# Softmax probabilities divided by their row sums on VectorE before they are turned, in a fused attention and mixture-of-experts layer

## The reference

```python
x = x + attn(layernorm(x))       # 16 heads, latent rank 64, rotary part 64
x = x + ffn(layernorm(x))        # 8 experts, 2 per token, and a shared one

# attn, per sequence b and head h
scores  = einsum('bthd,bshd->btsh', q, k) * SCALE
weights = softmax(scores, axis=2)            # over s
attn    = einsum('btsh,bshd->bthd', weights, v)
out     = attn.reshape(b, s, NH * DV) @ Wout
```

## Time and profile before

| | us |
|---|---|
| median of 3 runs (632.36 to 633.71) | 633.29 |
| the profiled execution's own time | 640.3 |
| its span (first to last instruction) | 638.6 |
| PE busy in the span | 611.4 (96%) |
| DVE busy | 469.9 (74%) |
| ACT busy | 474.8 (74%) |
| POOL busy | 410.1 (64%) |
| mean granted TensorE clock | 0.974 |

### The profile page before, as it was taken

The page is one execution under the profiler, slowest core; times in us unless marked ns, Lnnn a source line. Parts: engine busy times, 40 slices in busy tenths (PEclk is TensorE's granted clock), DMA queues, the critical chain, the costliest instruction groups (busy, mean ns, idle before and its releaser), DMA issues. The chain is left out here.

```text
span 638.6 us, 15728 instructions
## 1 busy us (share of the span) xinstructions
PE 611.4 (96%) x4916; PEld 596.4 (93%) x4916; DVE 469.9 (74%) x1406; ACT 474.8 (74%) x1331; POOL 410.1 (64%) x455
## 2 busy tenths in 40 slices
PE   9988999999999999999999999999988889999995
PEld 8878999999999999899999999999978879999994
DVE  6666787877886888778688788778755666666486
ACT  4669899898998989779898898979854335565531
POOL 1466797786897889679789988978603204444500
PEclk9997999999999999999999999999989689999997
DMA  9891000000001001000100100011403055444292
GB/s 254 254 332 29 2 1 3 2 2 34 10 10 42 10 18 44 8 16 5 43 18 10 43 9 19 34 53 43 149 1 133 33 152 166 131 119 133 77 316 87
DMA packets 34024, 45.41 MB, mean 71 GB/s; under 512 B 4056, under 2 KB 29112, under 8 KB 33944
## 3 DMA queue, kind: packets, MB, share of 16 engines
q1 hardware_dynamic: 29160, 34.56, 17.2%
q0 software_dynamic: 3408, 9.34, 4.5%
q10 hardware_dynamic: 1376, 0.50, 0.3%
HBM read 27.57 MB, written 16.82 MB: 70 GB/s over the span
## 5 line engine op out<-in xcount | busy, mean ns | idle before, releaser
L1244 ACT ACTIVATE probs<-ps_s,nmax 128x256 f32<-128x256 f32 x256 | 118.9, 475 | 14.4 <-DVE nmax L1434 14.3
L1779 POOL TENSOR_TENSOR qswap<-qswap,qsin 128x512 f32<-128x512 f32 x64 | 83.2, 1300 | 45.6 <-ACT qswap L1221 45.6
L226 PE MATMUL ps_q<-xa,wq_hi 128*128 128x256 f32 x512 | 101.0, 295 | 4.3 <-DVE qf L1429 4.3
L1434 DVE TENSOR_REDUCE nmax<-ps_s 128x2 f32<-128x512 f32 x128 | 86.9, 679 | 11.1 <-PE ps_s L226 10.6
L1221 ACT ACTIVATE pT_hi<-ps_t 128x512 fp32r<-128x512 f32 x128 | 76.6, 598 | 19.6 <-PE ps_t L978 18.2
L1782 POOL TENSOR_TENSOR qf<-qf,qswap 128x512 f32<-128x512 f32 x64 | 82.7, 1293 | 12.9 <-DVE qf L1429 8.9
L1786 POOL TENSOR_TENSOR q_lo<-qf,q_hi 128x512 fp32r<-128x512 f32 x64 | 83.0, 1297 | 6.7 <-ACT q_hi L1221 6.6
L226 PEld LDWEIGHTS ps_q<-xa,wq_hi 128*128 128x128 f32 x512 | 79.9, 192 | 6.0 <-DVE qf L1429 4.0
L299 DVE TENSOR_TENSOR pT_lo<-ps_t,pT_hi 128x512 fp32r<-128x512 f32 x128 | 81.9, 681 | 0.0
L226 PE MATMUL ps_s<-kT_hi,q_hi 128*128 128x256 f32 x256 | 78.3, 306 | 2.1 <-ACT probs L1244 2.1
L978 PE MATMUL ps_t<-ident,probs 128*128 128x128 f32 x512 | 78.0, 275 | 1.3 <-DVE pT_lo L299 1.2
(11 more groups left out here) (337 smaller groups left out, 1924.1 us busy)
## 6 DMA issues: line engine op xcount, KB each, us to landing
xg<-routed_in SPq DMA_DIRECT2D x39, 129.0 KB
normal_turned<-xf SPq DMA_DIRECT2D x8, 512.0 KB, 2.8
wq_raw<-Wq_dram SPq DMA_DIRECT2D x16, 192.0 KB, 4.6
x<-x_dram SPq DMA_DIRECT2D x8, 256.0 KB, 4.9
xa<-normal_turned SPq DMA_DIRECT2D x4, 512.0 KB, 4.8
mgu_hi<-routed_out SPq DMA_DIRECT2D x4, 512.0 KB, 5.2
mgu_lo<-routed_out SPq DMA_DIRECT2D x4, 512.0 KB, 8.0
out_dram<-x SPq DMA_DIRECT2D x8, 256.0 KB, 2.9
```

The source lines that it names most:

```text
L226: last = nc.tensor.matmul(out, stat, mov, start=start and n == 0, stop=stop and n == len(terms) - 1, skip_group_check=skip)
L1244: last = nc.scalar.activation(probs[h % 3][:, j, :], L.ps_s[h % 2][:, j, :], ACT.Exp, bias=nmax[:, h % NH, j:j + 1], accum_out=rsum[:, h % ...
L1434: vec.tensor_reduce(nmax[:, h % NH, :], L.ps_s[h % 2][:, :, :], AX.X, ALU.max, negate=True).then_inc(ev.max_done, 1)
L1779: gp.tensor_tensor(qs, qs, L.qsin[:, :].unsqueeze(1).to_broadcast([P, 2, S]), ALU.mult).then_inc(ev.qrot_part, 1)
```

## The change

`spread`, `norms` and `norm_out` fall away, and with them the tiles rinv and norm. A new function `scale(h)` on DVE multiplies the probabilities of a head in place, before PE turns them, by the reciprocal of each row's sum, which now is one number per partition. `scale` is two TENSOR_SCALAR operations of 128 x 256 in SBUF (one per tile of tokens), so four per pair. `turn(h)` waits for `scaled` in place of `exp_done`. `attended` is now a plain copy of ps_o to on, made by ACT; its place on ACT is behind `exps(2g+1)`. The first `attend` of a pair waits for `on_done` of the pair before.

```diff
             def turn(h):
-                pe.wait_ge(ev.exp_done, h + 1)
+                pe.wait_ge(ev.scaled, h + 1)
                 if h >= 2:
                     pe.wait_ge(ev.plo_done, h - 1)
...
                 pe.wait_ge(ev.plo_done, h + 1)
-                if n == 0:
-                    pe.wait_ge(ev.norm_done, g + 1)
+                if h == 0:
+                    pe.wait_ge(F.wlo_done, NH)
+                if n == 0 and g >= 1:
+                    pe.wait_ge(ev.on_done, g)
...
-            def norms(g):
-
-                if g == 0:
-                    pe.wait_ge(F.wlo_done, NH)
-                pe.wait_ge(ev.rinv_done, g + 1)
-                if g >= 1:
-                    pe.wait_ge(ev.on_done, g)
-                for j in range(NT):
-                    last = nc.tensor.transpose(L.ps_o[:, 1, tile(j)], rinv[g % 2][:, j, :, :].rearrange("p n c -> p (n c)"), L.ident[:, :])
-                last.then_inc(ev.norm_full, 1)
...
-            def norm_out(g):
-                act.wait_ge(ev.norm_full, g + 1)
-                if g >= 1:
-                    act.wait_ge(ev.on_done, g)
-                copy(norm[:, :], L.ps_o[:, 1, :]).then_inc(ev.norm_done, 1)
+            def attended(g):
+                act.wait_ge(ev.pv_done, 2 * g + 2)
+                if g >= 2:
+                    act.wait_ge(ev.olo_done, g - 1)
+                copy(on[g % 2][:, :], L.ps_o[:, 0, :]).then_inc(ev.on_done, 1)
...
-            def spread(g):
-
+            def scale(h):
+
+                g, n = divmod(h, 2)
                 dve.wait_ge(ev.small_inv, g + 1)
-                if g >= 2:
-                    dve.wait_ge(ev.norm_full, g - 1)
-                vec.tensor_reduce(rinv[g % 2][:, :, :, :].rearrange("p j n c -> p (j n) c"),
-                                  rinv_1[g % 2][:, :, :].rearrange("p j n -> p (j n)").unsqueeze(2).unsqueeze(3).to_broadcast([P, 2 * NT, RANK, 1]),
-                                  AX.X, ALU.max).then_inc(ev.rinv_done, 1)
+                for j in range(NT):
+                    last = vec.tensor_scalar(probs[h % 3][:, j, :], probs[h % 3][:, j, :], rinv_1[g % 2][:, j, n:n + 1], None, ALU.mult)
+                last.then_inc(ev.scaled, 1)
...
-            def attended(g):
-                dve.wait_ge(ev.pv_done, 2 * g + 2)
-                dve.wait_ge(ev.norm_done, g + 1)
-                if g >= 2:
-                    dve.wait_ge(ev.olo_done, g - 1)
-                vec.tensor_tensor(on[g % 2][:, :], L.ps_o[:, 0, :], norm[:, :], ALU.mult).then_inc(ev.on_done, 1)
...
                 if pair(g + 3):
                     query_cos(g + 3)
-                if pair(g - 2):
-                    attended(g - 2)
                 inverse(g)
                 if pair(g + 1):
                     maxima(2 * (g + 1))
-                spread(g)
+                scale(2 * g)
+                scale(2 * g + 1)
                 if pair(g - 1):
                     probs_lo(2 * (g - 1))
                     probs_lo(2 * (g - 1) + 1)
```

More of the change, by code:

```diff
@@ L75, in __init__ @@
             sem, ("q_full", "qraw_done", "qcos_done", "qrot_part", "qrot_done", "qhi_done", "qlo_done"))
-        self.small_inv, self.rinv_done, self.norm_full, self.norm_done, self.on_done, self.ohi_done, self.olo_done, self.out_done = map(
-            sem, ("small_inv", "rinv_done", "norm_full", "norm_done", "on_done", "ohi_done", "olo_done", "out_done"))
+        self.small_inv, self.scaled, self.on_done, self.ohi_done, self.olo_done, self.out_done = map(
+            sem, ("small_inv", "scaled", "on_done", "ohi_done", "olo_done", "out_done"))
         self.s_full, self.max_done, self.exp_done = map(sem, ("s_full", "max_done", "exp_done"))
@@ L797, in loop @@
             rinv_1 = [at(f"rinv_1{n}", [P, NT, 2]) for n in range(2)]
-            rinv = [at(f"rinv{n}", [P, NT, 2, RANK]) for n in range(2)]
-            norm = at("norm", [P, S])
             on = [at(f"on{n}", [P, S]) for n in range(2)]
@@ L1149, in _ @@
                     query(g + 4)
-                if pair(g - 1):
-                    norms(g - 1)
                 if pair(g + 1):
@@ L1162, in _ @@
             project(PAIRS - 3)
-            norms(PAIRS - 1)
             attend(HEADS - 2)
@@ L1350, in _ @@
                 exps(2 * g + 1)
+                if pair(g - 2):
+                    attended(g - 2)
                 if pair(g + 2):
@@ L1358, in _ @@
                     exps(2 * (g + 1))
-                if pair(g - 1):
-                    norm_out(g - 1)
                 if r == 4 and batch(i - 1):
@@ L1377, in _ @@
                 probs_hi(2 * g)
+            attended(PAIRS - 2)
             probs_hi(HEADS - 1)
             attended_hi(PAIRS - 2)
-            norm_out(PAIRS - 1)
+            attended(PAIRS - 1)
             silu(0, 0)
@@ L1439, in inverse @@
                 if g >= 2:
-                    dve.wait_ge(ev.rinv_done, g - 1)
+                    dve.wait_ge(ev.scaled, 2 * g - 2)
                 vec.reciprocal(rinv_1[g % 2][:, :, :], rsum[:, 2 * p:2 * p + 2, :].rearrange("p n j -> p j n")).then_inc(ev.small_inv, 1)
-            def spread(g):
+            def scale(h):
+                g, n = divmod(h, 2)
                 dve.wait_ge(ev.small_inv, g + 1)
-                if g >= 2:
-                    dve.wait_ge(ev.norm_full, g - 1)
-                vec.tensor_reduce(rinv[g % 2][:, :, :, :].rearrange("p j n c -> p (j n) c"),
-                                  rinv_1[g % 2][:, :, :].rearrange("p j n -> p (j n)").unsqueeze(2).unsqueeze(3).to_broadcast([P, 2 * NT, RANK, 1]),
-                                  AX.X, ALU.max).then_inc(ev.rinv_done, 1)
+                for j in range(NT):
+                    last = vec.tensor_scalar(probs[h % 3][:, j, :], probs[h % 3][:, j, :], rinv_1[g % 2][:, j, n:n + 1], None, ALU.mult)
+                last.then_inc(ev.scaled, 1)
             def probs_lo(h):
@@ L1696, in _ @@
                     maxima(2 * (g + 1) + 1)
-            attended(PAIRS - 2)
             probs_lo(HEADS - 2)
@@ L1701, in _ @@
             masks(B - 2)
-            attended(PAIRS - 1)
             unit_lo(0, 0)
```

## The result

The changed kernel takes 726.44 us (median of 4 runs, 725.83 to 728.19), beside 633.50 for the kernel before in the same session: a ratio of 1.144 [1.1395, 1.1485]. It is slower by 93 us; 714 was predicted, in a range from 622 to 745.

The account below looks back on a forecast made before the run. PE was taken to bound the loop before, DVE after: 3.63 own round + 1.08 scales + 1.73 waits = 6.44 us, 63 times, plus 91.8 = 497.5, 81 above 416.5; 640.3 + 81 = 721, less 7.0 gives 714 us, range 622 to 745.

Parts of the forecast that it names:

- A scale of 0.27 us from start to start: On DVE: 0.21 for a CAST-like operation plus 0.06 for the per-partition factor, 1.08 us a round.
- Waits of 1.73 us a round: DVE's scales wait for POOL's rotate 0.21, query_lo 1.25, attended_lo 0.70, less 0.43 of issue; chance 0.65.
- the upper bound: Scales' waits on DVE: 3.0 us a round, if one more POOL operation of 1.3 us gets in.
- The term for `attended_lo`, 0.70: On DVE: the third scale of a round waits 0.70 us for POOL's attended_lo, which follows query_lo at once.
- the lower end of 0.95 us a round: Scales' waits for POOL without the third, giving 665 us, the low end of the turn-taking case's own range.
- DVE's loop of 497.5 us: Attention loop on DVE: 63 rounds of 6.44 us plus 91.8 of other sequences' pieces, 81 above 416.5.
- PE waits at `turn`, 1 to 2 us a round: Expected sign in the profile after: PE waits for DVE before turn, one to two us a round.
- The mean of a scale, about 0.75 us: Expected sign on DVE: 256 TENSOR_SCALAR averaging about 0.75 us, some of 1.3 to 1.5 ending with a POOL operation.
- The final step, 721 less 7 us: Whole kernel: profiled execution 640.3 + 81 = 721, taken as 7.0 above the median, so 714 us.
- The rival "out of the fast mode": On DVE: the per-partition factor prevents the fast mode, no meeting with POOL, 1.56 us a round; 630 us, chance 0.15.
- the room of 1.52 us: On DVE: scales may take 1.52 us a round, waits included, before the loop exceeds the earlier 416.5 us.
- The gain as built, 13.3 us: PE saves 0.21 us a round from norms, 13.3 us in all, with the rest hidden; 620 us.

Follow-up runs that it names:

- no division: The changed kernel without scale, turn waiting for small_inv and the probabilities left undivided; 616.02 us, ratio 0.9699.
- POOL short: The changed kernel with POOL's rotate and query_lo operations cut to 8 columns a head, the rest left out; 625.11 us, ratio 0.984.
- sums written: The changed kernel with each scale also writing its row sum into a tile nobody reads; 661.37 us, ratio 1.0425.
- sums written, ahead of query_cos: The changed kernel with row-sum-writing scales of heads 2g-1 and 2g first in DVE's round, a reciprocal per head; 659.51 us, ratio 1.0397.
- plain, ahead of query_cos: The changed kernel with its scales, for heads 2g-1 and 2g, moved ahead of query_cos, a reciprocal per head; 672.34 us, ratio 1.056.
- sums written, in the gap: The 661.37 us kernel with scale(2g-1) behind query_cos, scale(2g) behind maxima(2g+2), a reciprocal per head; 667.16 us, ratio 1.0495.
- sums written, split: The 661.37 us kernel with scale(2g) ahead of maxima(2g+2) and scale(2g+1) behind it; 672.26 us, ratio 1.0586.
- plain, at the round's end: The changed kernel with its scales, for heads 2g+1 and 2g+2, moved to the end of DVE's round ahead of maxima(2g+3); 691.39 us, ratio 1.088.
- query_lo short: The changed kernel with only POOL's query_lo cut to 8 columns a head, the rest left out; 668.11 us, ratio 1.0528.
- attended_lo short: The changed kernel with only POOL's attended_lo cut to 8 columns, the rest left out; 705.08 us, ratio 1.1108.
- one TENSOR_TENSOR a head: The changed kernel with one 128 x 512 TENSOR_TENSOR per head, factors read with step 0, replacing two TENSOR_SCALAR; 721.01 us, ratio 1.1351.
- plain, in the gap: The changed kernel's scales without sums, scale(2g-1) behind query_cos, scale(2g) behind maxima(2g+2), a reciprocal per head; 732.90 us, ratio 1.1533.

## Why the prediction was right, step by step

The forecast was slower, and the mechanism that it named is the one that the runs show; the size of the sum came out right in part by errors that cancelled. The kernels can be laid side by side by the scales' busy time a round (times as measured; the kernel before took 633.5 to 636.6 us beside them):

| kernel | scales, us a round | us |
|---|---|---|
| no division | 0 | 616.0 |
| POOL short | 1.18 | 625.1 |
| sums written | 1.67 | 661.4 |
| sums written, ahead of query_cos | 1.68 | 659.5 |
| plain, ahead of query_cos | 1.71 | 672.3 |
| sums written, in the gap | 1.74 | 667.2 |
| sums written, split | 1.75 | 672.3 |
| plain, at the round's end | 1.78 | 691.4 |
| query_lo short | 1.80 | 668.1 |
| attended_lo short | 2.47 | 705.1 |
| one TENSOR_TENSOR a head | 2.60 | 721.0 |
| the change | 2.79 | 726.4 |
| plain, in the gap | 3.13 | 732.9 |

- **A scale of 0.27 us from start to start.** Right: four free ones take 1.14 us, three pitches of 0.27 and a last record of 0.34.
- **Waits of 1.73 us a round.** Measured 1.65. The mechanism is shown by the three kernels that take it away (another form, POOL short, `query_lo` short), and in the round above it stands as it was drawn: the rest of the rotate, `query_lo`, `attended_lo`, one free. But the composition was not that in every round. In the timelines `query_lo` begins inside 53 of the 64 trains of four (58 with those that it precedes by less than 0.2 us, which is how the expectation of the `query_lo` run counts) and `attended_lo` inside only 29, while 16 trains hold one more half of a rotate, which I had only in the upper bound. The term for `attended_lo`, 0.70, came to 0.32; that the extra rotates about made up for it was not tried, but in any case this sum was partly luck. Two of its figures were also off in the working: half of 0.27 three times is 0.41, not 0.43, and the lower end of 0.95 us a round is not "without the third wait", which by the same sum leaves 1.2.
- **DVE's loop of 497.5 us.** Measured 503.2, but made up otherwise. The sum held 461.6 us of work and one gap a round, before `inverse`, of 1.77 - 1.20 = 0.57 us, or 35.9 in all. The gap is there, 35.0 us before the RECIPROCAL, but DVE is busy for only 446.0: from start to start the scales hold 169.4 us where the sum had 177.0, and all else 276.6 where it had 284.6. Against these 16 us less stand 22 us of idle time that the sum put at nothing, before `query_cos` and `maxima` above all. So the 5.7 us between 497.5 and 503.2 are the rest of two larger errors.
- **PE waits at `turn`, 1 to 2 us a round.** 72.6 / 63 = 1.15. ACT's and POOL's shares fell, as foreseen. PE's granted clock fell from 0.99 to 0.97 in the loop, and with it PE's busy time rose from the 406.9 of the form without waits (clock 1.00) to 419.3. PE has idle time to cover it, so I put nothing on it.
- **The mean of a scale, about 0.75 us.** 0.757, with some at 1.3 to 1.46.
- **The final step, 721 less 7 us.** This one failed. The profiled execution of the kernel before lay 7.0 above its median; that of the kernel after is 726.82, level with its median of 726.44. The offset belonged to that one execution and should not have been carried over. Outside the loop the two executions take the same (640.3 - 416.5 = 223.8 and 726.8 - 503.2 = 223.6 us), so it probably lay in the loop of before, which the sum had replaced. Of the 12 us missed, 7 are here and 6 in the loop, less 1 of rounding.
- **The rival "out of the fast mode".** Its mechanism didn't occur, but the form that writes sums is as good as that case: no waits, 1.60 us a round where I had 1.56. I gave it 630 us, and it took 661. From the first `attend` to the last it needs 438.3 us (shown with its run), where DVE's sum gives 63 x 5.23 + 91.8 = 421. The step that failed here is the room of 1.52 us. I let DVE fill up to PE's 416.5 without asking what is late meanwhile; the two kernels at 1.67 and 1.68 are 27 and 25 above the kernel before. The one with POOL short (1.18) is below it, but POOL is relieved there too, so how much room there really is was not measured. Moving the scales gained where they had waited for POOL (726 to 672 and 691 us), but no place brought them clearly below the 661: before `query_cos` the rotate is late, ahead of a maxima the exps are, at the end (tried with plain scales only) both the exps and `pT_lo`, and in the gap the turn has its scale in its own round. What share each of these chains has in the 27 us is not settled.
- **The gain as built, 13.3 us.** Without the division it is 19. In the trace of before, `norms` and what the first matmul behind them takes longer make 14.0 us of the loop from start to start, near the 13.3. PE's idle time in the loop fell as well, from 417.5 - 410.2 = 7.3 us between the same ends before to 395.3 - 392.2 = 3.1 without the division. Which of the removed waits that is was not tried. `attended` and `spread`, 0.66 us of DVE a round, and ACT's wait for `norms`, 14.0 us (another 14.0), also go.

## What to carry to other kernels

Before work is moved to VectorE, look at what GpSimd does at that place: several short VectorE operations in SBUF in a row, beside a row of long GpSimd operations, can each wait for one of GpSimd's. Here four operations of 0.34 us took 2.79 us a round instead of 1.14. Of the 112 us between a gain of 19 and a loss of 93, the form that doesn't wait gives 64 back. Where they can't be avoided, a form that doesn't wait may be the faster one though it is slower alone (0.40 us from start to start against 0.27, 661 us against 726); and in a tight cycle of five engines the room on one can be less than its idle time: the sum gave the scales 1.52 us a round, and with four of 0.40 us each, 1.60 us without a wait for POOL, the kernel was already 27 us slower than before.

## What the hardware showed that I had not expected

- The two engines took turns, instruction by instruction: of two scales queued back to back the second did not keep its place against a GpSimd operation that had become ready meanwhile (316.50 on POOL, 316.61 to 317.99 on DVE). The scale then waited for the whole operation, and 156 of the 168 stretched ones in this kernel end just behind one of POOL's.
- A TENSOR_SCALAR with a factor per partition and accumulation took 467 to 480 ns at any time, without it 338 to 1458 (256 of each in two kernels that differ in nothing else).
- A TENSOR_TENSOR of two SBUF sources, one of them a single column repeated, waits as well: 678 to 1787 ns. There GpSimd's `query_lo` waited too, 1.73 us at the median and not 1.29.
- One order of plain scales (in the gap) was slower than the change, though it moved them to where DVE had been idle, because the operation ahead of them releases the GpSimd operation that they then meet. There the granted clock of PE was 0.94 in the loop.
